# Second attention of a two-layer tower: zeroing exponentials on GpSimd in place of mask products, and value products three or four steps later

## The reference, cut to what matters

```python
windows = jnp.array([max(4, BLOCK_SIZE // 2 ** h) for h in range(H)], dtype=jnp.int32)
...
mask = (j <= i)[None] & (j > i - windows[:, None, None])
att = jnp.einsum('bhtd,bhsd->bhts', q, k) * (1.0 / math.sqrt(D))
att = jnp.where(mask[None], att, -jnp.inf)
att = jax.nn.softmax(att, axis=-1)
out = jnp.einsum('bhts,bhsd->bhtd', att, v)
combined = out.transpose(0, 2, 1, 3)
gates = jax.nn.softmax(x @ Wgate + bgate, axis=-1)
gated = (combined * gates[..., None]).reshape(Bx, Tx, C)
return gated @ Wproj + bproj
```

## Time and profile before

| | us |
|---|---|
| median of 3 runs (lowest, highest) | 1427.9 (1424.0, 1430.46) |
| the profiled execution, its own time | 1427.86 |
| its span, first to last instruction | 1426.1 |
| first product of the second attention | 669.36 |
| last instruction of it (normalisation) | ends 801.88 |
| TensorE busy in 669 to 810, of 141 us | 121.8 |

### The profile page before, as it was taken

The page is one execution under the profiler, slowest core; times in us unless marked ns, Lnnn a source line. Parts: engine busy times, 40 slices in busy tenths (PEclk is TensorE's granted clock), DMA queues, the critical chain, the costliest instruction groups (busy, mean ns, idle before and its releaser), DMA issues. The chain is left out here.

```text
span 1426.1 us, 29279 instructions
## 1 busy us (share of the span) xinstructions
PE 1232.4 (86%) x9695; PEld 967.0 (68%) x9696; DVE 849.3 (60%) x1794; ACT 650.3 (46%) x1253; POOL 666.0 (47%) x616
## 2 busy tenths in 40 slices
PE   6886999999978959972899796999689999989996
PEld 3664555555546747761667584999668888878885
DVE  5997788888827948996555494744323333333332
ACT  3881666666655635430354463333123333333332
POOL 7855777777361213787100000455225545444553
PEclk9995899999999977775999998999889999999998
DMA  2588999999400006563444320011275343545331
GB/s 56 172 255 264 253 273 276 278 282 270 111 2 1 1 28 184 173 202 94 91 113 95 110 83 30 23 30 37 68 268 133 55 110 80 139 129 137 51 53 19
DMA packets 122867, 179.27 MB, mean 126 GB/s; under 512 B 26052, under 2 KB 83820, under 8 KB 122772
## 3 DMA queue, kind: packets, MB, share of 16 engines
q1 hardware_dynamic: 105876, 159.62, 38.4%
q0 software_dynamic: 16896, 18.44, 7.9%
HBM read 104.73 MB, written 74.31 MB: 126 GB/s over the span
## 5 line engine op out<-in xcount | busy, mean ns | idle before, releaser
L1635 DVE TENSOR_REDUCE att_top<-att_psS 128x4 f32<-128x512 f32 (+2 forms) x192 | 195.2, 1037 | 46.8 <-PE att_psS L1522 43.7
L2791 POOL DMA_INDIRECT out<-ffn1c_y,ffn1c_table x72 | 113.3, 1574 | 180.8 <-ACT ffn1c_y L2904 92.1
L2932 DVE TENSOR_TENSOR ffn1c_hid<-ffn1c_psG,ffn1c_sil 128x512 f32<-128x512 f32 x72 | 49.8, 692 | 146.5 <-PE ffn1c_psG L2832 146.5
L1606 ACT ACTIVATE att_prob<-att_psS 128x1024 f32<-128x1024 f32 (+1 forms) x96 | 83.3, 888 | 64.9 <-PE att_psS L1536 64.9
L1516 PE MATMUL att_psS<-pairs_ka,pairs_qa 48*128 48x384 f32 (+3 forms) x512 | 100.3, 400 | 12.3 <-DMA pairs_ka<-k_parts 7.8
L2832 PE MATMUL ffn1c_psG<-ffn1c_w_h,ffn1c_xh 128*128 x288 | 97.9, 422 | 11.6 <-DMA ffn1c_w_l<-experts_lo 5.7
L1606 ACT ACTIVATE pairs_part<-att_psS 128x1024 f32<-128x1024 f32 (+1 forms) x96 | 82.8, 888 | 35.5 <-PE att_psS L1536 35.5
L2435 POOL DMA_INDIRECT slots<-ffn1b_entry,ffn1b_sloti x64 | 63.3, 989 | 65.7 <-ACT ffn1b_act_h L2648 54.1
L2780 POOL DMA_INDIRECT ffn1c_rows<-normed_rows,ffn1c_table x72 | 71.1, 987 | 45.4 <-DVE ffn1c_gate L2952 21.3
L2832 PE MATMUL ffn1c_psG<-ffn1c_w_l,ffn1c_xh 128*128 x288 | 91.5, 399 | 0.0
L2832 PE MATMUL ffn1c_psG<-ffn1c_w_h,ffn1c_xl 128*128 x288 | 91.3, 399 | 0.0
(11 more groups left out here) (397 smaller groups left out, 3505.4 us busy)
## 6 DMA issues: line engine op xcount, KB each, us to landing
prep_raw<-in_w_all SPq DMA_DIRECT2D x27, 512.0 KB, 5.4
experts_hi<-ffn0w_room SPq DMA_DIRECT2D x27, 512.0 KB, 5.6
experts_lo<-prep_lo SPq DMA_DIRECT2D x27, 512.0 KB, 6.6
ffn1c_w_h<-experts_hi SPq DMA_DIRECT2D x8, 1536.0 KB, 7.0
ffn1c_w_l<-experts_lo SPq DMA_DIRECT2D x8, 1536.0 KB, 11.4
qkv_near<-near_keys SPq DMA_DIRECT2D x32, 320.0 KB, 4.3
q_parts<-pairs_part SPq DMA_DIRECT2D x8, 1024.0 KB, 4.1
k_parts<-pairs_part SPq DMA_DIRECT2D x16, 512.0 KB, 5.9
```

Source lines behind the costliest of these rows:

```text
L1606: act.activation(dst, src, ACT.Exp, scale=0.25).then_inc(s["exp"], 1)
L1635: dve.tensor_reduce(dst, src, AX.X, ALU.max).then_inc(s["max"], 1)
L2791: pool.indirect_dma_start(out=rows_out, in_=y[:, t.buf, :], in_offset=None, out_offset=bass.IndirectOffsetOnAxis(ap=table[:, t.value:t.val ...
L2932: dve.tensor_tensor(hid[:, t.par, :], psG[:, t.par, 1, :], sil[:, t.par, :], ALU.mult).then_inc(s["act"], 1)
```

## The change

It has two parts. In `events`, PV no longer opens the stage but stands behind A1: after TOP, before the steps 4 to 7. And for the heads with 64 keys and more (windows 256, 128, 64; called `wide`), the key side's mask products go: the exponentials are taken of unmasked scores, and GpSimd writes zeros where the query lies outside of the head's window, by two `affine_select` instructions per head and unit, one for the near edge (the query is older than the key) and one for the far edge (the query is more than the window away). A new semaphore `cut` counts them; PV waits for it beside `exp`. Where a key tile has fewer queries than the slot is wide and the window is 128 or 64, one narrower mask product stays; where the window is 256, the exponential now takes only the columns that exist (256 and 128 in place of 384 for the last two tiles). The eight bias additions on GpSimd move from the start to behind the selects of each even unit.

```diff
@@ events @@
     steps, out = out, []
-    if (u - 3).exists():
-        out += [("PV", 0)]
     out += steps[:3]
     if (u - 1).exists():
         out += [("TOP", 0)]
-    out += steps[3:8]
+    out += steps[3:4]
+    if (u - 3).exists():
+        out += [("PV", 0)]
+    out += steps[4:8]
     if (u - 3).exists():
         out += [("OUT", 0)]
@@ attend, GpSimd @@
+        wide = [[(h, w) for h, w in enumerate(g) if w >= P // 2] for g in windows]
+        cuts = [2 * len(g) for g in wide]
...
-            for b in range(B):
-                r = res[:, TG * b:TG * (b + 1), :]
-                pool.tensor_tensor(r, r, bias[:].unsqueeze(1).to_broadcast([P, TG, D]), ALU.add).then_inc(s["biased"], 1)
+            def stage(u):
+                v = u - 2
...
+                for h, w in wide[v.hg]:
+                    last = max(q for q, sl in enumerate(key_slots(windows, v.hg)) if sl[0][1] == h)
+                    pool.wait_ge(s["exp"], v.slots(nb, last + 1))
+                    near = prob[:, v.par, h, :, 0:P]
+                    pool.affine_select(out=near, in_=near, compare_op=ALU.is_ge, fill=0.0, base=0, pattern=[[0, TG], [1, P]],
+                                       channel_multiplier=-1).then_inc(s["cut"], 1)
+                    n += 1
+                    tiles = sum(S - P * j > w for j in range(TG))
+                    if w < P:
+                        pool.wait_ge(s["cut"], v.slots(cuts, n))
+                    far = prob[:, v.par, h, 0:tiles, w:w + P]
+                    pool.affine_select(out=far, in_=far, compare_op=ALU.is_gt, fill=0.0, base=0, pattern=[[0, tiles], [-1, P]],
+                                       channel_multiplier=1).then_inc(s["cut"], 1)
+                    n += 1
+                if v.hg == 0:
+                    r = res[:, TG * v.seq:TG * (v.seq + 1), :]
+                    pool.tensor_tensor(r, r, bias[:].unsqueeze(1).to_broadcast([P, TG, D]), ALU.add).then_inc(s["biased"], 1)
@@ attend, TensorE, key_tile @@
+                if (h, w) in wide[u.hg]:
+                    if have < cols and w <= P:
+                        pe.matmul(out[:, have:cols], idb[:], mask_k[w][:, have:cols], start=True, stop=True, skip_group_check=True)
+                    return pe.matmul(out[:, 0:have], keys, qs, start=True, stop=True, skip_group_check=True)
@@ PV @@
                         pe.wait_ge(s["exp"], v.slots(nb, nb[v.hg]))
+                        pe.wait_ge(s["cut"], v.slots(cuts, cuts[v.hg]))
@@ ScalarE @@
                         if len(sl) == 1:
+                            cols = min(cols, S - P * j)
```

More of the change, by code:

```diff
@@ L1119, in attend @@
         s_load, s_values = ([k.sem(f"{name}{n}") for n in range(2)] for name in ("load", "values"))
-        names = "const scoresA max topT_ps topT m_out m_in scoresB exp pv outT turned rec norm biased".split()
+        names = "const scoresA max topT_ps topT m_out m_in scoresB exp cut pv outT turned rec norm biased".split()
         s = {n: k.sem(n) for n in names}
@@ L1125, in window @@
             return windows[u.hg][h] if windows else None
+        wide = [[(h, w) for h, w in enumerate(g) if w >= P // 2] for g in windows]
+        cuts = [2 * len(g) for g in wide]
         @block.gpsimd
         def _(pool):
-            for b in range(B):
-                r = res[:, TG * b:TG * (b + 1), :]
-                pool.tensor_tensor(r, r, bias[:].unsqueeze(1).to_broadcast([P, TG, D]), ALU.add).then_inc(s["biased"], 1)
+            def stage(u):
+                v = u - 2
+                if not v.exists():
+                    return
+                n = 0
+                for h, w in wide[v.hg]:
[15 more added lines that the diff above has]
+                    pool.tensor_tensor(r, r, bias[:].unsqueeze(1).to_broadcast([P, TG, D]), ALU.add).then_inc(s["biased"], 1)
+            for n in range(2, NU + 2):
+                stage(Unit(n, None, groups))
             pool.wait_ge(s["biased"], B)
```

## The result

The changed kernel takes 1438.55 us (median of 5 runs, 1437.47 to 1440.62) against 1427.9 before: a ratio of 1.0089, 95% interval 1.0072 to 1.0105. The profiled execution took 1440.62 us, its span is 1438.9. The second attention runs from 670.36 to 816.11, that is 145.75 us against 132.52 before; its +13.2 is a little more than the whole difference of the spans, 12.8.

What follows compares the result with a forecast made beforehand. TensorE was taken to pace the second attention. A pair of 12.4 + 2.3 + (0.24 to 0.66) gives +0.6 to +3.2 us over six pairs; with -3.6, 1424.9 to 1427.5, said as 1426, range 1411 to 1431.

Steps and rivals of the forecast that it cites:

- the hold: Even stages: GpSimd's bias addition holds VectorE's tiny gates product; TensorE stands still 2.3 us once a pair of stages.
- the lost clock: Behind each hold TensorE runs at half speed for 4 us, adding some 2 us; the forecast itself counted none.
- rival 2: Second attention: the hold also makes TensorE lose its clock; +10 us in all, 1438; chance 0.10.
- Part 1: Mask products taken off TensorE in the second attention: 1.39 us a pair of stages, taken as 1.3.
- Part 2: Value products placed behind A1 no longer wait for the last exponential: 1.2 us a pair come back.
- step (a): Exponentials behind the value products come late: replaces like waits in even stages, costs some 0.2 us in odd ones.
- Step (b): TOP waits for the normalisation: about 0.24 us in the even stage, up to 0.66 with a select's hold in the odd.
- Step (c): GpSimd against VectorE: addition starts some 0.05 us ahead of the gates product and holds it, TensorE losing 2.3 us a pair.
- E: End of B2's exponential in the even stage; A3's maximum was put at E + 4.8, TensorE ready at E + 2.6.
- Step (d): SyncE's queue of loads and maxima: a pair cannot run faster than some 13.1 us, 13.1 to 13.4 by the queue.
- Filling and draining: First and last stages: mask products of two pairs (2.6) and two waits (1.0) go, -3.6 us.
- Rival 1: VectorE's gates product gets in ahead of the addition, no hold: a pair of 13.3, 1415 (1411 to 1419); chance 0.37.

Runs made afterwards that it cites:

- e8: e7 with SyncE's six loads of the next unit issued between the maxima going out and coming back in: 1442.89 us, ratio 1.0112.
- e6: Changed kernel with each bias addition as two instructions of two tiles: 1425.14 us, ratio 0.9981.
- e10: Changed kernel with each bias addition as two instructions, of three tiles and of one: 1428.37 us, ratio 1.0009.
- e11: Changed kernel with 3 idle TensorE products in front of odd stages' A0, where e2 has 13: 1432.89 us, ratio 1.0042.
- e4: Changed kernel with the eight bias additions ahead of all selects and the value products back at the stage's start: 1424.23 us, ratio 0.9974.
- e1: Changed kernel with the reciprocals written to PSUM, so the gates product has one SBUF input instead of two: 1416.3 us, ratio 0.9928.
- e5: Kernel before the change with only the value products (PV) moved behind A1: 1422.49 us, ratio 0.9982.
- e9: e7 with only the values' load issued while the maxima are in flight, the six loads staying in front: 1416.0 us, ratio 0.9927.
- e2: Changed kernel with 13 idle TensorE products in front of odd stages' A0, filling the standstill: 1430.11 us, ratio 1.0023.
- e7: Changed kernel with reciprocals in PSUM and the eight bias additions ahead of all selects: 1417.09 us, ratio 0.9941.

## Why the prediction was wrong, by its own steps

The prediction said 1426, 1411 to 1431, with the hold in its forecast and the lost clock as rival 2, priced at 1438 and given 0.10. What happened is rival 2: the hold, as forecast, and the lost clock on top of it.

**The step that failed** is the forecast's term for what follows the hold: it put the lost clock at nothing, and gave the reason in rival 2: "The hold's 2.3 us lie between, near the one that kept the clock." It drew a line between two waits, 2.27 kept and 3.1 lost, and decided "from a stall of about 3 us on". The runs show 1.76 us a pair for this term, and no such line at these lengths. In the changed kernel standstills of 2.16 to 2.19 us lost the clock in each of the six pairs of the middle. In e8, around the waits shown above, those of 2.10 and 2.20 lost it and those of 2.07 and 1.89 kept it. The granted clock of e8 behind 720.75, 737.58, 754.35 and 788.39:

```profile
723.00:725.00 2.00, 2.00 (x19) 1.18 (x13) 0.38 (x1) 0.00 (x0) 0.00 (x0) 0.50 0.13 36
740.00:742.00 2.00, 2.00 (x16) 0.99 (x11) 0.21 (x1) 0.00 (x0) 0.00 (x0) 0.50 0.26 67
755.00:757.00 2.00, 2.00 (x28) 1.35 (x26) 1.89 (x4) 0.87 (x2) 0.00 (x0) 1.00 0.00 0
789.00:791.00 2.00, 2.00 (x28) 1.35 (x27) 1.86 (x4) 0.87 (x2) 0.00 (x0) 1.00 0.00 0
```

Waits of 1.99 at 770.46 and of 2.25 at 695.03 of e8 lost it too. So with the 2.27 of the earlier trace rows there are both outcomes from 1.9 to 2.3 us, and of all standstills up to 1.7 (e6, e10, e11) none lost it. One kept instance was no evidence for safety at that length, and the chance of 0.10 was far too low. What decides between the two outcomes at 2 us is open; the changed kernel lost it behind all six such standstills of its trace. Rival 2 expected a loss at shorter stalls only between sparse products, but TensorE was busy for the whole of the 2.2 us ahead of the one that ended at 740.03, and of the 2 us behind it.

**The other terms:**
- Part 1, mask products. 112 of them remain as said (16 of L1254, 96 of L1256). Over five whole pairs TensorE's busy time a pair fell from 13.58 before (67.92 us from 704.67 to 778.89) to 12.51 in e4 (62.57 us from 706.12 to 777.49), by 1.07 where 1.3 was taken. With the value products moved as well it is 12.67 in e1 (63.37 us from 703.04 to 771.22), 0.91 less than before; e5 shows the other 0.2 as well (13.78).
- Part 2, value products. Their wait is gone as said. The 1.2 us came back only in part, since step (a) was wrong: it found B4's wait for B2's exponential (0.43 by its numbers; 0.46 in the changed kernel at 735.20, 2.9 us in 7 times in all), and then let it replace "like waits of before", but before had none in the middle of the stage beside the value products' own. Short waits for the maxima's DMA add 0.3. In e1 TensorE stands idle for 0.96 a pair, where 1.26 was idle before, so a pair without hold is 13.64, not 12.6 to 13.1.
- Step (b), TOP behind the normalisation: 0.32 to 0.34 and 0.56 in turn, with the select's hold (0.66 said). In e1, without a hold, no such wait is listed; the 0.24 did not appear.
- Step (c), the hold: right in mechanism, place and order. The addition led by 0.20 us at 736.34 and 0.07 at 718.99, where 0.05 was said. A0 waited 2.16 to 2.19 for 2.3 said (its own E + 4.8 less E + 2.6 is 2.2). By the port rule of the Trainium skill ("SBUF — State Buffer", section "SBUF: two separate sides"), whoever starts first has the pair for the whole instruction, against a VectorE instruction with two SBUF inputs. The trace agrees: 2.18 us with two such inputs, 0.17 with one (e1), 1.10 when the instruction ahead is half as long (e6).
- Step (d): the queue as a floor of 13.1 to 13.4. e9 does not bear it out as the pace: with time returned to the queue the pair did not move.
- The clock: 1.76 a pair for 2 said. Filling and draining: +0.9 up to the first group 0 value products and -3.4 from the last, together -2.5 for -3.6 said (in e1, without the hold, it is -4.2).

The sum by what was measured: 6 pairs from 691.58 to 796.50 take 104.92, before 89.21, so +15.7; with -2.5 that is +13.2, the second attention's +13.2. Rival 2's +10 came from smaller waits (0.3 a pair for the 0.95 that e2 shows) and more for filling and draining. That the median came out on its 1438 is in part luck: the two traced executions are 12.8 us apart, the medians 10.7.

Rival 1 (no hold, 1415) is what e1, e7 and e9 show: 1416.3, 1417.1 and 1416.0. This too is in part luck: its pair of 13.3 was 0.3 too short, and its -3.6 for filling and draining too small. **e1 beats both kernels**; e9 has the same time, and its interval overlaps with that of e1.

## What to carry to other kernels

Before GpSimd gets work beside VectorE, list VectorE's instructions with two SBUF inputs that stand on a chain, however tiny: one of 0.17 us was held for 2.2. Put one of its inputs in PSUM, or keep the GpSimd instructions that can be ahead of it short. And price a new standstill of TensorE in the range where the trace shows a kept and a lost clock by both outcomes; one that kept it proves little, and here the lost clock (1.76 a pair) cost nearly as much as the wait (2.18).

## What was not expected of the hardware

- TensorE's clock was lost behind standstills of 1.99, 2.10 and 2.16 to 2.25 us, and kept behind 1.89, 2.07 and 2.27.
- The fall comes before or after work resumes: in e8 the products from 737.58 on run at the full clock at first, and the mean falls to 0.56 only in the stretch from 739 to 740, while behind the wait that ended at 770.46 the first product (256 columns) already took 0.39 us in place of 0.28. The changed kernel shows the same with standstills of one length, 2.17 and 2.18 us. Where A0 resumed at 705.25, the clock was still full up to 706, and where it resumed at 774.75, the mean from 774 to 775 was 0.66, which is full clock for only the first 0.32 us of it, so that the fall came before A0:

```profile
705.00:706.00 1.00, 0.75 (x9) 0.68 (x10) 0.83 (x2) 0.00 (x0) 0.00 (x0) 1.00 1.06 288
...
774.00:775.00 1.00, 0.25 (x3) 0.25 (x4) 1.00 (x2) 0.00 (x0) 0.00 (x0) 0.66 0.76 236
```

- A waiting VectorE instruction goes in at the seam of two GpSimd additions that run back to back (ends 729.64, additions 728.35 to 730.84), so that cutting a GpSimd instruction in two halves its hold at once.
